# Preparations merged into attention's block, one transpose for the routing weights, and reordered copies and sums

## What is computed

```python
mod = (silu(c) @ wmod).reshape(16, 6, 1, 128)
sa, ca, ga, sb, cb, gb = (mod[:, j] for j in range(6))   # ga, gb: magnitude at least 0.25
h = layernorm(x) * (1 + ca) + sa
q, k, v = h @ W_Q, h @ W_K, h @ W_V                       # 16 heads of 64
probs = softmax(causal(q k^T / 8))
x = x + ga * (einsum(probs v, W_out) + b_out)
h = layernorm(x) * (1 + cb) + sb
logits = h @ Wr + br                                      # 8 experts
weights = softmax(logits where logits >= second largest, else -inf)
y = sum_e weights[:, e] * (gelu(h @ W1[e] + b1[e]) @ W2[e] + b2[e])
x = x + gb * y
```

## Time and profile before

| | us |
|---|---|
| median of three runs | 2071.55 (2071.41 to 2072.11) |
| profiled execution, whole | 2071.85 |
| its span, first to last instruction | 2070.0 |
| TensorE busy | 1998.7 (97% of the span) |
| VectorE busy | 1686.3 (81%) |
| ScalarE busy | 1574.4 (76%) |
| GpSimd busy | 729.0 (35%) |

### The profile page before, as it was taken

One profiled execution on the slowest core, in us unless ns is written; L12 is line 12 of the kernel. 1 busy time (PEld: TensorE's weight loads), 2 busy tenths in 40 slices (PEclk: granted clock), 3 DMA queues, 4 the chain that ended last, 5 costly groups with the idle time before them and its releaser, 6 DMA issues. The chain is left out here.

```text
span 2070.0 us, 46464 instructions
## 1 busy us (share of the span) xinstructions
PE 1998.7 (97%) x12751; PEld 1552.8 (75%) x12751; DVE 1686.3 (81%) x4518; ACT 1574.4 (76%) x3765; POOL 729.0 (35%) x1215
## 2 busy tenths in 40 slices
PE   5999999999999999999999999799999999999998
PEld 4777777777777777777777776588888888888887
DVE  5887777887877877877877877698888899888897
ACT  4888788788878888878788877567777777777775
POOL 2444444444444444444444443022222222222222
PEclk9999999999999999999999999899999999999999
DMA  4000000000000000000000000411112111111111
GB/s 110 22 1 1 0 0 0 0 0 0 0 0 0 0 0 0 0 0 0 0 0 0 0 1 1 123 47 47 46 48 75 55 46 51 46 46 46 46 62 35
DMA packets 41932, 49.46 MB, mean 24 GB/s; under 512 B 3176, under 2 KB 23712, under 8 KB 41888
## 3 DMA queue, kind: packets, MB, share of 16 engines
q1 hardware_dynamic: 41632, 48.41, 7.6%
q0 software_dynamic: 256, 0.53, 0.2%
HBM read 44.47 MB, written 4.46 MB: 24 GB/s over the span
## 5 line engine op out<-in xcount | busy, mean ns | idle before, releaser
L353 POOL TENSOR_SCALAR probs<-probs,rdenom 128x512 f32<-128x512 f32 (+3 forms) x1024 | 529.0, 538 | 693.3 <-DVE rdenom L724 693.3
L590 ACT ACTIVATE probs<-probs,neg_max 128x256 f32<-128x256 f32 (+3 forms) x1024 | 562.9, 552 | 132.4 <-DVE neg_max L715 131.4
L715 DVE CUSTOM_DVE_ANT_0 probs<-banks,mask_w 128x256 f32<-128x256 f32 (+3 forms) x1024 | 434.1, 487 | 102.8 <-PE banks L415 100.7
L1042 ACT ACTIVATE hidden<-banks,b_cols 128x512 f32<-128x512 f32 x512 | 348.4, 685 | 198.9 <-PE banks L908 173.4
L1161 DVE TENSOR_TENSOR hid_lo<-hidden,hid_hi 128x512 fp32r<-128x512 f32 x512 | 386.4, 763 | 68.1 <-ACT hid_hi L1050 55.7
L708 DVE COPY probs_T<-banks 128x512 f32<-128x512 f32 x384 | 260.0, 677 | 111.6 <-PE banks L441 109.2
L441 PE MATMUL banks<-ident,probs 128*128 128x128 f32 x2560 | 340.4, 275 | 2.1 <-DVE z_lo L728 1.5
L980 POOL TENSOR_TENSOR acc<-acc,y_w 128x512 f32<-128x512 f32 x112 | 155.4, 1387 | 489.9 <-DVE y_w L1174 489.9
L441 PEld LDWEIGHTS banks<-ident,probs 128*128 128x128 f32 x2560 | 288.3, 141 | 48.1 <-DVE neg_max L715 19.2
L456 PE MATMUL banks<-probs_T,v_sb 128*64 128x512 f32 (+3 forms) x2048 | 303.9, 439 | 1.6 <-DVE probs_T L708 1.6
L456 PEld LDWEIGHTS banks<-probs_T,v_sb 128*64 128x64 f32 x2048 | 135.6, 136 | 148.4 <-issue 118.9
(11 more groups left out here) (140 smaller groups left out, 3412.7 us busy)
## 6 DMA issues: line engine op xcount, KB each, us to landing
w_rows<-w_kept SPq DMA_DIRECT2D x128, 256.0 KB, 4.1
x_all<-in_L_attn_resid_dram SPq DMA_DIRECT2D x16, 256.0 KB, 2.8
out_dram<-y_result SPq DMA_DIRECT2D x16, 256.0 KB, 2.3
w_raw<-in_L_ffn_W_dram SPq DMA_DIRECT2D x12, 256.0 KB, 5.0
hidden<-in_L_ffn_W_dram SPq DMA_DIRECT2D x4, 256.0 KB, 6.2
v_sb<-in_L_attn_W_Q_dram SPq DMA_DIRECT2D x1, 512.0 KB, 6.1
v_sb<-in_L_attn_W_K_dram SPq DMA_DIRECT2D x1, 512.0 KB, 7.8
v_sb<-in_L_attn_W_V_dram SPq DMA_DIRECT2D x1, 512.0 KB, 11.5
```

The lines of the kernel that those rows point to most:

```text
L353: pool.tensor_scalar(part, part, rdenom[:, p % 2, 4 * h + r:4 * h + r + 1], 1.0, ALU.mult, ALU.mult)\
L590: act.activation(part, part, ACT.Exp, bias=neg_max[:, p % 2, col:col + 1], scale=-1.0, accum_out=denom[:, p % 2, col:col + 1]).then_inc(p_ ...
L715: dve.tensor_tensor_reduce(out=probs[:, p % 2, h, at:at + n], in0=S_BANK[u][h][:, col:col + n], in1=mask_w[:, 512 - n:512], scale=-SCALE, ...
L1042: act.activation(hidden[:, e % 2, c, :], banks[:, c, :], ACT.Gelu, bias=b1_cols[:, e * HC + c:e * HC + c + 1]).then_inc(hid, 1)
```

## The change

1. **One block for preparations and attention.** The first block is gone; its work stands at the head of attention's block in each engine's program. SyncE loads `c` first, then `x`, `wmod`, the weights, and `b1` and `b2` last. TensorE now transposes `c`, then the normed rows of batch 0, then multiplies `wmod`. ScalarE and VectorE split the weights one at a time among the first steps: `W_Q` and `W_K` before the first scores, `W_V` and the gates in step 0, `W_out` at the end of step 0. The scratch tiles moved so that they lie in `probs[:, 1]`.
2. **ScalarE's order in a step.** Copies of units 1 and 3 (`evac_T`) now stand before the last two exponentials and ahead of `h_evac`, `round_h` and the value copies; the very last exponential (128 columns) comes after the value copies.
3. **VectorE's order in a step.** The sums of pair p are inverted in step p+1, after its first two maxima, so GpSimd's products start there too. Unit 4 is copied right after unit 2. `ln_apply` is cut in two halves, at p = 3 and p = 4, ahead of the copy of unit 0.
4. **The last value chunk of a batch** moves on TensorE from the end of step 7 to the start of the next batch's body, behind the jump back of the loop.
5. **The routing weights** are packed 128 by 32 and transposed once instead of four times; `w_T` is 32 by 128, and `w_kept` is written from 32 partitions. GpSimd's clearing of `w_now` is gone.
6. **`sum_T`** moves from e = 1 to e = 2, the addition to `x` (`finish`) with it, behind `norm_rows`; `norm_T` waits for it at e = 3, since both use one bank.

The diff, cut to its core:

```diff
+                    dve.wait_ge(c_ps, 1)
+                    dve.tensor_copy(c_cols, g_bank[:, 0:B]).then_inc(c_ok, 1)
                     ln_stats(0)
+                    dve.wait_ge(exp_c, 1)
+                    link(dve.tensor_scalar(e1_c, e_c, 1.0, None, ALU.add))
+                    link(dve.reciprocal(sig_c, e1_c))
...
+                    dve.tensor_tensor(silu_c, c_cols, sig_c, ALU.mult).then_inc(silu_ok, 1)
                     ln_apply(0)
+                    dve.wait_ge(mod_ps, 1)
+                    link(dve.tensor_copy(mod_cols[:, :, :].rearrange("p j b -> p (j b)"), s_banks[0][:, 0:6 * B]))
...
+                    split_weights(0)
                     rest_h(0)
+                    split_weights(1)
                     rest_q(0, 0)
                     rest_k(0, 0)
...
...
+                        if not first:
+                            values(b - 1, NP - 1, 0, 8)
                         for p in range(NP):
...
+                            if first and p < 2:
+                                pe.wait_ge(w_split, 3 + p)
...
-                            if now:
+                            if now and p < 7:
                                 values(b, p, 0, now[-1])
...
-                            exponentials(b, p, 1, 1)
                             if not begin:
                                 evac_T(*prev, 1, first and p == 1)
-                            if len(now) > 1:
-                                values_out(b, 1, now[0])
+                            exponentials(b, p, 1, 1, [2])
+                            if not begin:
+                                evac_T(*prev, 3, False)
                             if p == 5 and not last:
                                 h_evac(b + 1)
                             if p == 6 and not last:
                                 round_h(b + 1)
-                            if not begin:
-                                evac_T(*prev, 3, False)
+                            if len(now) > 1:
+                                values_out(b, 1, now[0])
                             if now:
                                 values_out(b, 0, now[-1])
+                            exponentials(b, p, 1, 1, [0])
...
                             mask_and_max(b, p, 1, 2)
+                            if not begin:
+                                invert_sums(*prev)
                             mask_and_max(b, p, 0, 0)
...
+                            if begin:
+                                split_weights(2)
+                                gates()
...
+                            if p in (3, 4) and not last:
+                                ln_apply(b + 1, (2 * p - 6, 2 * p - 5))
...
                                 evac_T(*prev, 2, False)
-                            if p == 3 and not last:
-                                ln_apply(b + 1)
+                                evac_T(*prev, 4, False)
                             if p == 4 and not first:
                                 add_attention(b - 1)
-                            invert_sums(b, p)
-                            if not begin:
-                                evac_T(*prev, 4, False)
...
+                            if begin:
+                                split_weights(3)
...
-                        for t in range(NT):
-                            mm = pe.transpose(wT_bank[:, t * P:(t + 1) * P], w_now[:, t, :], ident[:, :])
-                        mm.then_inc(r_wT_ps, 1)
+                        pe.transpose(wT_bank[0:NT * E, 0:P], w_now[:, :, :].rearrange("p t e -> p (t e)"), ident[:, :])\
+                            .then_inc(r_wT_ps, 1)
...
-                            if e == 1 and not first:
+                            if e == 2 and not first:
                                 sum_T(b - 1)
                             if not last and e == 3:
+                                if not first:
+                                    pe.wait_ge(y_out, b)
                                 norm_T(b + 1)
```

260 lines of the change are left out of this document (131 added, 129 removed).

## The result

The changed kernel takes 2022.82 us, median of four runs (2021.87 to 2025.12), where the kernel before takes 2071.75 (2071.41 to 2072.11): 48.9 less, a ratio of 0.9765 (95% interval 0.975 to 0.978). The forecast was 2032 with a range from 2024 to 2043. So the sign was right and the gain too small: 39.5 us where 48.9 came. Five more runs, taken later, gave 2022.39 (2022.06 to 2024.62); I call their profile *the second profile*. It matters, because the two profiled executions of the same program differ by 3.1 us.

A forecast was written before the change was run, and what follows sets the result against it. The prediction took TensorE, busy 97% of the span, as the bound. Gains of 24.5 us in attention, 5.9 at the start and 9.1 in the experts made 39.5, so 2032 us, range 2024 to 2043.

The forecast's parts named there:

- ScalarE's order: Attention steps 0, 1, 2 and 6: earlier copies remove TensorE's waits before the first scores, 1.15 us a batch.
- the copies arrive no earlier: Rival in attention: TensorE waits there for something nearly as late, half of attention's gain is lost, 2045 us; chance 0.12.
- VectorE's order: Attention steps 4 and 5: waits of 0.47, 0.05 and 0.09 us go; 0.15 a batch charged for the moved reciprocal.
- 14 x (1.76 - 0.15): Attention's batches 1 to 14: waits of 1.76 us less the 0.15 charge, 22.5 gained; attention in all 24.5.
- The last pair: End of attention: the reciprocal behind unit 4's copy starts GpSimd's products later, costing 0.6 us once, between 0 and 0.9.
- The later normalisation: Attention's loop: inverting sums in the next step costs nothing; GpSimd's products for unit 0 keep 0.4 us of cover.
- the rival of slower products: GpSimd's products in attention, expected at 4.1 us, slow down beside VectorE; at 1.2 more, 2057 us; chance 0.03.
- The start: One block: first scores 11.2 us earlier, less 2.2 in step 0, 2.2 and 1.4 in step 1, plus 0.5: 5.9 gained.
- The experts: Experts' batches: fewer routing-weight transposes save 5.3 us, the later `sum_T` 3.8: 9.1 gained, 8 to 10.
- signs named for "right": Scores at 0.32 us in all steps, attention batches 1.6 shorter, first scores near 20, experts' batches 0.6 shorter, GpSimd's wait 5.
- "wrong": Signs: unit 0's transposes wait for GpSimd, a reciprocal waits for ScalarE, matmuls at 0.43 after 35 us, scores after 24.
- Every rival: Besides late copies and slower products: the start gives nothing (2037 us, chance 0.08); GpSimd becomes the bound (2083, 0.03).

The follow-up runs named there:

- act_old: The changed kernel with ScalarE's old order (last exponentials and `h_evac` ahead of the copies of units 1 and 3): 2042.51 us.
- ln_old: The changed kernel with `ln_apply` whole again in step 3 and unit 4 copied after it, the reciprocal left in the next step: 2032.66 us.
- loop_only: The kernel before with only ScalarE's and VectorE's new orders; two blocks, experts and last value chunk as before: 2041.45 us.
- invert_later: The changed kernel with the reciprocal one maximum later, behind the first 512-column one: 2057.21 us.
- start_only: The changed kernel with ScalarE's and VectorE's old orders, the value chunk back in step 7 and the old experts, so only the one block is new: 2061.07 us.
- experts_only: The kernel before with only one transpose for the routing weights and the sum's transposes at e = 2: 2062.00 us.
- gate_moved: The changed kernel with the second gate (four instructions and their waits) moved from step 0 to the tail of attention: 2102.91 us.
- v4: The changed kernel with a reordered start, second gate in attention's tail, first pair's sums inverted in step 0: 2097.23 us; with eight already met waits 2018.25.
- v5: v4 with the head of the experts in another order on VectorE and ScalarE: 2094.73 us; with eight already met waits 2015.33.

## Why the forecast was too small, step by step

I take the second profile, which is nearer to the median: 2022.06, that is 49.8 less than the profile of before and 10.3 more than the forecast gain. Of these, 6.5 are attention's orders, 3.8 the start, and none the experts.

- **ScalarE's order: right.** 1.15 a batch forecast, 1.17 shown by act_old. The copies come in time, and the rival "the copies arrive no earlier" fell.
- **VectorE's order: the place right, the size wrong.** This is the larger of the two steps that failed: "I charge 0.15 a batch" and the sum 14 x (1.76 - 0.15). The loop's batches became 1.99 shorter, 0.38 more than that. The charge doesn't exist. The reciprocal pushes `ln_stats` in step 2 from 4.08 to 4.14 after the scores' start, the later copy of unit 0 stays at 5.3, and that step got shorter by 0.04. And waits were counted only up to the matmul that waited: the earlier trace rows has the second group of step 4 at 619.37, but from there to its third pair of matmuls it takes 0.57 (619.94), where the changed kernel takes 0.46. The kernel before and ln_old both show the 0.10 twice, in steps 4 and 5, and that makes 0.20 a batch. Together 0.15 + 0.04 + 0.20 = 0.39, of the 0.38 found. Over attention: 31.0 instead of 24.5 (2.2 in batch 0, 41.1 - 11.9 = 29.2 behind it, less 0.4 at the end); loop_only, alone, gave 30.7.
- **The last pair: right.** 0.6 forecast; the lead falls from 38.12 at the last pair's scores to 37.70 at the experts' first transposes in the changed kernel's profile, so 0.42.
- **The later normalisation: right.** No wait for GpSimd in the loop, and invert_later finds the cover of 0.4. The products take 4.11, beside VectorE's maxima and copies, so the rival of slower products fell. The Trainium skill ("GPSIMD Engine Reference", Specifications) has GpSimd contend with some of VectorE's instructions for SBUF; here they took 4.08 beside an almost idle VectorE, so that is at most 0.03.
- **The start: terms of the sum mis-sized.** This is the other step that failed. 5.9 forecast. In the second profile the lead at batch 1 is 105.42 - 93.56 = 11.86, of which the new orders gave 1.8 in steps 3 to 7 and 0.4 in step 2. The prediction had counted that return (0.5) for the start, but loop_only has it (8.76 instead of 9.15) and start_only doesn't (9.15). That leaves 9.7 for the start. The first scores led by 12.3, not 11.2: `h_evac` starts at 12.13 instead of 12.6, and the projection of k is held 0.13 by its split matrix instead of 0.6. Step 0 gave back 9.14 - 7.58 = 1.6 instead of 2.2, since the 7.58 of before were themselves at half pace (31.37 has a row of 0.58; loop_only had the same step in 6.64). Step 1 gave back 9.32 - 8.26 = 1.1 instead of 2.2 + 1.4: TensorE waits 2.06 for GpSimd, its first transposes come 4.2 after the step's start and not 5.0, and nothing slow follows. In the other profile the slow matmuls came (33.73 to 37.2), as forecast, and step 1 took 1.7 more; the other 1.25 between the profiles are its slow first scores in step 0. The forecast took one state of the clock as given in a place where it varies from one execution to the next.
- **The experts: right.** 9.1 forecast; 49.8 less the lead of 1279.51 - 1238.41 = 41.1 at the last pair's scores leaves 8.7, and with the 0.4 of the tail 9.1. Alone (experts_only) it was 10.1.

The attention term alone, 6.5 too small, would have left the time inside the range, and so would the start's 3.8; the two together are the miss.

Of the signs named for "right", all came true but the batch of the loop, which is 1.99 shorter and not 1.6. Of "wrong", two showed, both in step 1 of batch 0: unit 0's transposes wait for GpSimd there (1.32 and 2.06), and one of the two profiles has matmuls at 0.43 after 35 us, for 1.7 us. Neither decided. Every rival fell for this kernel. But that nothing slowed the loop was luck. The prediction has no term for where VectorE's loop lies in the code, and the changed kernel starts it at 338, where a start at 331 costs 80 us (gate_moved): a slower result lay one small edit away, by a mechanism that no rival named.

## What to carry to other kernels

Count a wait on TensorE from the last undisturbed start to the first undisturbed distance behind it. In the second score group here the matmul that waited costs another 0.10, even after a wait of 0.01; in the first group it costs nothing more, so look at each place. An order on one engine and the place of a dependent step on another may be one edit; test them apart before keeping half. And compare each batch of a loop, the first one too, after any edit ahead of the loop: four small instructions moved out of the way cost 80 us, and in v4 and v5 eight idle waits got 79 back.

## What the runs showed of the hardware that I had not expected

**The jump of a loop.** VectorE's loop of 366 instructions had no wait at its jump when it started at instruction 337, 338, 339 or 468 of its program. The first maximum came 4.1 later at 331, and 1.9 later at 498. The Trainium skill ("Runtime: NRT & Kernel Launch", Instruction fetch mechanics) says that most engines hold their code in two blocks of 256 instructions, and that a taken branch to code outside them has to fetch it first. The runs agree: an edge just behind 331 and at 337 at the latest puts the loops that waited across three blocks and the others in two. The page gives no price for it. Here it was 6.0 us in each of 13 batches at 331 and 1.8 at 498. The first price holds about 1.7 of slow matmuls, since TensorE's clock fell behind the longer idle time; the second holds none. Why VectorE itself stops for 4.1 in one place and 1.9 in the other stays open.

**The clock.** The same program, with the same 1.3 us of idle time before it, ran its first scores at 0.43 a matmul in one profile and at 0.23 in another. The granted clock of the stretch reads 1.00 in both, and only the next stretch tells them apart. The kernel before has the same: 1.00 from 31.3 to 33.0, with matmuls of 512 columns at 0.43. Windows of the changed kernel, then of the second profile (the window and its length, busy time of PE, PEld, DVE, ACT and POOL, granted clock, DMA share, GB/s):

```profile
19.00:29.00 10.00, 7.47 (x36) 5.74 (x36) 7.12 (x30) 7.46 (x22) 0.00 (x0) 1.00 0.35 104
29.00:38.00 9.00, 7.15 (x39) 6.23 (x40) 6.40 (x21) 5.04 (x16) 4.12 (x8) 0.62 0.31 91
```

```profile
19.00:29.00 10.00, 6.19 (x46) 4.77 (x48) 8.18 (x29) 7.61 (x22) 0.00 (x0) 1.00 0.33 100
29.00:38.00 9.00, 6.94 (x58) 5.87 (x56) 7.11 (x23) 7.26 (x20) 4.09 (x8) 1.00 0.23 64
```

In the second stretch a part ran at the lower level (1.2 GHz, mean 0.62) in the first profile and none in the other. What decides which it is, no run here tells.
